# A gated cross-attention block in fp32 on one core: the first steps of stage 2 moved into attention's last block, and even score chunks

## The reference

```python
# x: (2, 2048, 512), context: (2, 77, 512); every product in fp32
h = layernorm(x)
z = self_attn(h, Wq1, Wk1, Wv1)        # one head, 2048 keys, causal, padding mask
x1 = layer_norm(h + z, ln1_g, ln1_b)
z = cross_attn(x1, ctx, Wq2, Wk2, Wv2) # 77 keys, mask by the count of non-zero scores in row 0
x2 = layer_norm(x1 + z, ln2_g, ln2_b)
z = relu(x2 @ fc1_w + fc1_b) @ fc2_w + fc2_b
x = x + tanh(g_xattn) * layer_norm(x2 + z, ln3_g, ln3_b)
# then the gated feed-forward with quantised weights: 512 -> 2048 -> 512, silu
x = x + tanh(g_ffn) * (x + 0.5 * ffn(layernorm(x)))   # ffn(...) as in the reference
```

## Time and profile before

| | |
|---|---|
| time, three runs | 1670.34, 1670.76, 1672.56 us |
| median | 1670.76 us |
| the profiled execution, its own time | 1670.44 us |
| its span in the profile | 1668.6 us |
| PE busy | 98% of the span |
| DVE, ACT, POOL busy | 51%, 34%, 22% |
| mean granted clock | 0.995 of full speed |
| chain that ended last | PE 91%, DVE 4%, POOL 2% |

### The profile page before, as it was taken

How to read it: one execution, slowest core, us unless ns; L and a number is a source line. 1 busy time by engine, 2 the same in 40 slices (tenths; PEclk the granted TensorE clock), 3 DMA queues, 4 the chain that set the end, 5 groups by cost and what they waited for, 6 DMA issues and landing times.

```text
span 1668.6 us, 20672 instructions
## 1 busy us (share of the span) xinstructions
PE 1636.9 (98%) x7746; PEld 1340.8 (80%) x7746; DVE 845.5 (51%) x1720; ACT 568.8 (34%) x990; POOL 368.9 (22%) x562
## 2 busy tenths in 40 slices
PE   8999999999999999899999899999999999999999
PEld 6887888877788888687878688888888888888887
DVE  6767443476664444688888955232333232333311
ACT  5432121134221212565566433232223222322322
POOL 1212101022210100488888801000000000000000
PEclk9999999999999999899999999999999999999999
DMA  6302110131221104554555432101010101010000
GB/s 210 105 22 95 44 51 26 40 114 57 70 76 39 38 26 140 163 165 152 164 164 158 126 115 69 45 1 51 1 51 1 51 1 51 1 51 1 26 1 26
DMA packets 66760, 116.19 MB, mean 70 GB/s; under 512 B 11185, under 2 KB 11185, under 8 KB 66507
## 3 DMA queue, kind: packets, MB, share of 16 engines
q1 hardware_dynamic: 64336, 110.36, 20.6%
q10 hardware_dynamic: 2325, 4.51, 0.8%
HBM read 80.00 MB, written 34.84 MB: 69 GB/s over the span
## 4 chain that ended last, share of the span: by engine, by line
PE 91%; DVE 4%; POOL 2%; issue 1%; ACT 1%; DMA 0%; SPq 0%; DVEq 0%; ACTq 0%
PE banks L694 86%; PE banks L704 3%; PE banks L881 2%; DVE split L1622 1%; DMA plain<-in_L_xattn_Wk 0%; POOL small L1486 0%; POOL split L1498 0%; DVE plain L1952 0%; DVE plain L1974 0%; POOL split L1505 0%; ACT plain L1193 0%; DVE split_q L1622 0%; ACT split L1086 0%; DVE plain L2156 0%; DVE plain L1662 0%
## 5 line engine op out<-in xcount | busy, mean ns | idle before, releaser
L694 PE MATMUL banks<-split_q,split 128*128 128x512 f32 x2328 | 571.3, 394 | 4.5 <-POOL split L1498 3.2
L694 PE MATMUL banks<-split 128*128 128x512 f32 (+4 forms) x2304 | 545.8, 386 | 9.6 <-DVE split L1622 6.5
L694 PEld LDWEIGHTS banks<-split_q,split 128*128 128x128 f32 x2328 | 431.3, 188 | 95.7 <-POOL split L1498 4.1
L694 PEld LDWEIGHTS banks<-split 128*128 128x128 f32 (+3 forms) x2304 | 414.1, 186 | 108.8 <-DVE plain L1952 9.0
L694 PE MATMUL banks<-split,split_q 128*128 128x512 f32 (+2 forms) x1728 | 394.8, 381 | 4.9 <-DVE split_q L1622 2.3
L694 PEld LDWEIGHTS banks<-split,split_q 128*128 128x128 f32 x1728 | 306.1, 189 | 61.3 <-DVE split_q L1622 3.5
L1622 DVE TENSOR_TENSOR split<-banks,split 128x512 fp32r<-128x512 f32 (+5 forms) x232 | 146.0, 638 | 154.5 <-ACT split L1086 153.6
L2121 DVE TENSOR_TENSOR split<-plain,split 128x512 fp32r<-128x512 f32 x128 | 88.5, 691 | 257.1 <-ACT split L1399 257.1
L1086 ACT ACTIVATE split<-banks 128x512 fp32r<-128x512 f32 (+5 forms) x232 | 123.8, 557 | 247.8 <-PE banks L881 199.5
L1393 ACT ACTIVATE plain<-banks,small 128x512 f32<-128x512 f32 x128 | 88.0, 688 | 289.1 <-PE banks L694 289.1
L1622 DVE TENSOR_TENSOR split_q<-banks,split_q 128x512 fp32r<-128x512 f32 x68 | 46.6, 686 | 222.0 <-ACT split_q L1086 222.0
(11 more groups left out here) (155 smaller groups left out, 1256.5 us busy)
## 6 DMA issues: line engine op xcount, KB each, us to landing
plain<-in_x SPq DMA_DIRECT2D x64, 256.0 KB, 2.7
xo_scratch<-plain SPq DMA_DIRECT2D x32, 256.0 KB, 2.3
x_scratch<-plain SPq DMA_DIRECT2D x32, 256.0 KB, 2.0
plain<-x_scratch SPq DMA_DIRECT2D x32, 256.0 KB, 3.0
tile_x<-xo_scratch SPq DMA_DIRECT2D x32, 256.0 KB, 3.1
xg_scratch<-tile_x SPq DMA_DIRECT2D x32, 256.0 KB, 2.0
out<-plain SPq DMA_DIRECT2D x32, 256.0 KB, 2.1
tile_x<-x_scratch SPq DMA_DIRECT2D x28, 256.0 KB, 3.8
```

The lines of the kernel that those rows point to most:

```text
L694: mm = nc.tensor.matmul(out, left(c, l), right(c, r), start=start and c == 0 and (l, r) == PASSES[0], stop=stop and c == chunks - 1 and (l ...
```

## The change

Five things change. (1) `span_of(i, c)`: scores of blocks 4, 8 and 12 are made in chunks of equal width (2 x 320, 3 x 384, 4 x 416) and not in 512s and a 128. Turns and values keep their chunks of 512. (2) The last block's list is written anew: Y1 stands before V1, K and Y3 and the first half of P follow, the other half of P stands behind the first turn of tile 1, and new letters are added: F splits of six of the eight row groups of fc1_w and fc2_w, J parts of `b1_shift`, U `probs`' turn and low part, y for all four turns of tile 1, H the four `cross_values(0, k)` with `add_z(0, k)`. (3) fc1_w and fc2_w get buffers of their own in `raw` (dead columns of xT) and are both loaded early, from SP, between N of tile 0 and V2; N of tile 1 is loaded early too; the vector loads wait for tile 0's additions. (4) `cross_values(0, k)` uses banks 6 and 5, and the addition of row block 15 (`sum_rows`) comes behind the four `add_z`. (5) Behind the list, PE does `cross_scores(1)` and then the turns of x2 with two parts of `b1_shift` between them, ACT takes `hi_x2` between the squares and the norms, DVE does block 15's end between the `lo_x2`, and the first `step2` has `mlp_in(0, 1)` ahead of `turn_scores(1)`.

```diff
+def span_of(i, c):
+
+    if i % 4:
+        return c * 512, width_of(i, c)
+    w = (i + 1) * P // chunks_of(i)
+    return c * w, w
...
             order += [("T", i, 0), ("T", i, 1), ("R", i, 0), ("V", i, 0), ("C", i, 0), end[0], ("Y", i, 0), ("T", i, 2),
-                      ("V", i, 1), end[1], ("Y", i, 1), ("Y", i, 2), ("V", i, 2), ("T", i, 3), ("Y", i, 3),
-                      ("P", i, 0), ("P", i, 1), ("K", i, 0), ("y", i, 0), ("y", i, 1), ("G", i, 0), ("V", i, 3),
-                      ("A", i, 0)]
+                      ("Y", i, 1), ("V", i, 1), end[1], ("Y", i, 2), ("K", i, 0), ("Y", i, 3), ("P", i, 0),
+                      ("y", i, 0), ("P", i, 1), ("F", i, 0), ("T", i, 3), ("F", i, 1), ("J", i, 0), ("y", i, 1), ("G", i, 0),
+                      ("V", i, 2), ("F", i, 2), ("U", i, 0), ("F", i, 3), ("y", i, 2), ("V", i, 3), ("F", i, 4), ("F", i, 5),
+                      ("y", i, 3), ("J", i, 1)]
+            order += [("H", i, c) for c in range(C)]
...
+                        for n, name in enumerate(("fc1_w", "fc2_w")):
+                            sp.dma_start(fc_raw[n], a[f"L0_xattn_{name}"].rearrange("(c p) n -> p c n", p=P)).then_inc(
+                                fcw_in[n], 16)
                         sp.dma_start(V2[0:SC].rearrange("p c h n -> p (c h n)").bitcast(F32), v_dram).then_inc(
                             cross_in, 16)
...
                     if i == NB - 1 and b + 1 == B:
-                        sp.wait_ge(z_free, 2 + B * NB)
+                        sp.wait_ge(tp_full, TURNS["p", b, i, 3] + 1)
+                        for k in range(BT):
+                            load_n(1, 1, k)
+                        sp.wait_ge(z_free, 2 + B * NB + BT)
...
+            def cross_values(t, k):
+                if k == 0:
+                    pe.wait_ge(tp_free, 2 + probs_at(t) + 1)
+                pe.wait_ge(z_free, z2_at(t, k) - 1 if t else B * NB + 1 + max(k - 1, 0))
+                product(PS[:, z2_bank(t, k)], lambda _, h: PT2[0:SC, h, k * P:(k + 1) * P],
+                        lambda _, h: V2[0:SC, t // TPB, h, :], 1, z2_full)
...
-            turn_x1(1, 2)
-            turn_x1(1, 3)
-            pe.wait_ge(fcw_in[0], 16)
-            b1_shift(0)
-            turn_probs(0)
-            b1_shift(1)
+            cross_scores(1)
             b1_shift(2)
+            turn_x2(0, 0)
+            turn_x2(0, 1)
             b1_shift(3)
-            pe.wait_ge(cross_in, 16)
-            for k in range(BT):
-                cross_values(0, k)
-            cross_scores(1)
-            for k in range(BT):
-                turn_x2(0, k)
+            turn_x2(0, 2)
+            turn_x2(0, 3)
             pe.wait_ge(fcw_lo, C)
             pe.wait_ge(b1_ready, 1)
...
             square_z(0, 0)
             square_z(0, 1)
             norm_z(0, 0)
             square_z(0, 2)
             norm_z(0, 1)
+            hi_x2(0, 0)
             square_z(0, 3)
             norm_z(0, 2)
+            hi_x2(0, 1)
             norm_z(0, 3)
-            hi_x2(0, 0)
-            hi_x2(0, 1)
+            hi_x2(0, 2)
+            hi_x2(0, 3)
+            hi_fc(6)
+            hi_fc(7)
...
+            sum_rows(NB - 1)
             stats_z(NB - 1)
-            split_fc1(range(C))
-            for k in range(BT):
-                add_z(0, k)
+            lo_x2(0, 0)
+            lo_x2(0, 1)
             end_b(NB - 1)
+            lo_x2(0, 2)
             dve.wait_ge(b1_full, 1)
             nc.vector.tensor_tensor(b1x, b1x, PS[:, 4, 0:C], ALU.add).then_inc(b1_ready, 1)
+            lo_x2(0, 3)
+            lo_fc(6)
+            lo_fc(7)
```

227 lines of the change are left out of this document (121 added, 106 removed).

## The result

| | before | changed |
|---|---|---|
| median of the runs, us | 1672.63 (8 runs, 1670.34 to 1674.91) | 1667.11 (8 runs, 1665.19 to 1669.80) |
| profiled execution, us | 1670.44 (span 1668.6) | 1669.80 (span 1668.0) |
| ratio to before | | 0.9972, 95% interval 0.9963 to 0.9981 |

The changed kernel is 0.28% faster: 4.7 us by the ratio (5.5 between the medians), where 2.5 were forecast, and just past the 0.2% that a measurement of it can tell from nothing. The range, 1664.3 to 1671.5, holds the median, and 1668.3 is 1.2 above it. That it comes so near is in part luck: the forecast started from 1670.76, the median of three runs, and the eight runs of before have 1672.63. The base was 1.9 too low and the gain too small.

What follows compares the result with a forecast made beforehand. PE, busy 98% of the span, was taken as the bound. From 1670.76 us: -1.7 chunks, -1.9 earlier `mlp_in`, +0.7 loads, +0.4 clock, together -2.5, gave 1668.3; range 1664.3 to 1671.5.

Steps and rivals of the forecast that it cites:

- Chunks: Stage 1 scores: even chunks save 0.42 at block 8 and 0.44 at block 12, 1.7 us over both batches.
- The two prices: Score chunks at blocks 8 and 12: one of 384 columns costs 2.19 us, one of 416 costs 2.35.
- The walk through the block: Last block, engines followed in five steps from the first turn of x1: `mlp_in` starts 1.9 us earlier.
- the four places named: PE's waits in the last block: 1.1 before Y1, 1.0 before P's second half, 1.6 on the exponential, 1.3 on `add_z`.
- the tail: Fifth step, first turn of x2 to `mlp_in`: 7.1 us instead of 5.3, giving back 1.8 of the 3.7 gained.
- The loads: fc1_w and fc2_w ahead of y0's rows on SP's queue: cost 0 to 2.0 us, taken as 0.7.
- The clock: Half clock when `mlp_in` starts: 2.0 us lost instead of 1.6, so 0.4 added.
- The rival with 0.14: Clock falls earlier as well, already at the last block's cross values, costing 2.7: 1671.0 us; chance 0.14.
- third and fourth steps: Last block, queues before the softmax, then additions: waits of 1.6 and 1.3; 3.7 us gained by the first turn of x2.
- free narrow chunks: Rival on stage 1 scores: evening out saves nothing, or DVE's extra maximum eats the gain: 1670.0 us; chance 0.08.
- the waits did not close: Rival on the last block: waits close, 1.6 less at `turn_probs`, and `mlp_in` at full clock, 2.0 less: 1664.7 us; chance 0.30.
- late rows: Rival on tile 1's rows: y0 waits until 672.6, 7.3 us beyond the count: 1675.6; chance 0.06. Wrong-sign: DMA wait over 3.

Runs made afterwards that it cites:

- a2_changed_again: The changed kernel with no edit, a second profiled execution beside the first; span 1665.4 us.
- e12: e11 plus ten overwritten products of 512 columns in the waits between the turns of x2; ratio to before 0.9972, median 1667.47 us.
- e10: Changed kernel with the fc loads behind y0's rows and the tail's ACT and DVE order turned round; ratio to before 0.9980, median 1669.19 us.
- e8: Changed kernel with later fc loads and ten overwritten products in PE's waits from the third turn of x2 to `mlp_in`; ratio to before 0.9977.
- e11: e10 plus the last two rows of one-column matmuls moved from the tail into earlier waits of PE; ratio to before 0.9965, median 1665.66 us.
- e13: Changed kernel with later fc loads, masks K behind Y3 and fc1_w's splits behind the softmax's scores; ratio to before 0.9990, median 1670.11 us.
- e1_chunks_only: Kernel before with even score chunks for blocks 4, 8 and 12 and nothing else; ratio to before 0.9984, median 1668.95 us.

## Why the prediction was right

**Chunks**: 1.7 forecast, 2.7 (1.2 to 4.2) measured alone, 1.9 in the trace of stage 1 (514.86 and 513.00 from block 4's scores to the turns ahead of the last block, 135.80 to 650.66 and 135.58 to 648.58). The two prices were right to 0.02. The surplus in the trace is the price of back-to-back chunks (2.12, taken as 2.19, and 2.28, taken as 2.35). Block 4 gave nothing, as forecast, and lost 0.1 in one batch and 0.3 in the other. The reason that I had given for such a loss, DVE's extra maximum, is not it: DVE makes that at 142.52, when PE's values have started at 142.34. They wait for a low part that DVE starts at 141.51, only 0.13 earlier than before, at the end of its own chain, while PE's chunks began 0.22 earlier. A narrow chunk of 128 columns costs 108 ns a matmul, and evening it out pays. The Trainium skill (TensorE: Matmul & The Clock Gate, Back-to-back issue gap) gives N / 2.4 + 2.5 ns for the isolated gap, 56 at 128 columns, and 81 ns for a stream of pairs of a load and a matmul. The Trainium skill (TensorE: Matmul & The Clock Gate, LDWEIGHTS (loading the stationary operand)) gives P / 1.2 ns for the load alone, 107 ns for 128 columns. The measured 108 lies at the last of these, so the load may be what a narrow chunk pays for. That isn't shown: the trace of before has each of these loads (24 of them from 188.6 to 192.6) at 187 to 192 ns, longer than the spacing, and no run here took the loads away.

**The walk through the block**: the waits came at four of the four places named, at sizes of 1.07 (forecast 1.1), 0.73 where no late rows hide it (1.0), 1.10 (1.6) and 0.65 (1.3). So none was larger than forecast, while the starts behind the last three, counted from the first turn of x1 in a2_changed_again, came within 0.3: 9.4 (forecast 9.3), 16.9 (17.0) and 24.1 (24.3). The chain of DVE and ACT that ends these waits was walked rightly; PE's own work ahead of the last two had been priced 0.3 to 0.4 too short. The first turn of x2 came 29.32 behind the first turn of x1 in a2_changed_again, forecast 684.9 - 655.67 = 29.2; the tail took 7.00, forecast 7.1; `mlp_in` 36.32, forecast 36.3. In the profiled execution of the changed kernel itself it came at 39.03, because of the loads and the early half clock.

**The loads**: the first rows were forecast 9.9 to 10.9 behind the first turn of x1; they came 10.1 behind it in the changed kernel, 8.5 in a2_changed_again and 7.8 in the block alone. Cost 0.7 with bounds 0 to 2.0; the traces have 1.2, 0 and 0.

**The clock**: half clock at `mlp_in`, as forecast, in every trace of a kernel with the new block but e12's. The 24 products lost 7.61 - 5.75 = 1.9 in the changed kernel, 1.4 in its second trace, 2.9 in the block alone; forecast 2.0. The reading of rows behind it was less exact: I had counted eight one-column matmuls in the tail, where the timeline has 16 (two rows of 8), and had said that turns and one-column matmuls preceded both falls of before, where only turns and waits preceded the second. The rival with 0.14, that the clock falls at the cross values too, is what the profiled execution of the changed kernel shows (6.02 instead of 4.57, 1.4 us), and it cost about as much as the load. It is no property of the kernel: a2_changed_again is the same code and hasn't got it. So this rival was no alternative to the forecast but something that differs from one execution to the next.

**What the sum left out.** Between the traces of before and a2_changed_again (spans 1668.6 and 1665.4) the gain is 3.2 and not 2.5. It is made of 2.1 ahead of the first turn of x1 (forecast 1.7; 0.2 of the 2.1 were there before the first changed chunk), 1.9 from there to `mlp_in` (forecast 1.9 less 0.7 for the loads, which cost nothing here), 0.2 given back up to the eight turns (forecast 0.4, for the clock) and 0.6 given back behind them, which had no term.

By the means of many runs the gain is 4.3: 1672.0 for the 89 runs of before beside the experiments, 1667.7 for the 18 of the changed kernel. The 1.1 that this has over 3.2 lies in the profiled execution of before, which was a fast one: 1670.44, 1.5 below the mean, where a2_changed_again's 1667.25 is 0.4 below its own. The 25 of the 89 runs with its mean clock of 0.995 average 1671.7. The forecast was worked out from that execution.

The granted clock doesn't explain the 1.1. Time does go with it in the runs of before (18 at 0.993 average 1673.1 us and 16 at 0.996 average 1671.0, 0.7 us for each 0.001), and the changed kernel has 0.9963 over its 18 runs where before has 0.9943. But the two traces differ by the same 0.002 (0.995 and 0.997; 17.1 and 10.2 us of half clock in all), so what the higher clock is worth is already in the 3.2. It is in the forecast too, whose third and fourth steps take out the long low stretch of before. Adding it to the sum would count it twice. What makes a usual execution of before slower than its trace stays open, since no trace shows such a run.

Of the rivals, free narrow chunks are refuted; the waits did not close, and where experiments closed them the time came back at half clock or at the next wait; late rows stayed at 1.97 and did not reach the 3 us that would have made it wrong.

## What to carry to other kernels

Price a narrow chunk of a score row by its own rows in the trace: at 128 columns a matmul cost 108 ns here and at 512 it cost 237, so the same columns in equal pieces are cheaper, wherever no wait stands behind them. Before crediting a shortened wait ahead of a stretch of half clock, mark a point behind that stretch: 1.46 us gained at the first product were 0.04 us some 18 us later. Where the effect sought is a few tenths of a per cent, take a second trace of the same kernel before explaining a row: one wait of 1.97 and one of 0.30 had the same code. And take one of before as well: the only one here was 1.5 us faster than the mean of its kernel.

## What of the hardware was not expected

- The stretch of half clock at the MLP's entry kept its place when PE's work in it was changed: 32.5 to 34.0 us behind the first turn of x1 and 6.8 us long, with PE busy 4.38 (a2_changed_again), 5.39 (e10) or 6.41 us (e8) of it. The Trainium skill (TensorE: Matmul & The Clock Gate, Part 4: PE-mode transpose) says that turns don't count as busy for the clock in the way that products do. The traces fit that: turns, most often with one-column matmuls, preceded it in the kernels in which it stayed. Moving the one-column matmuls away with the tail's order (e11) or adding products (e8) left it. With all of these together (e12) one trace has it at two other places with the same total of 6.7 us. Whether the edit did that isn't shown: the two traces of the changed kernel also have it at different places (679.55 and 689.80 in one, 686.05 alone in the other).
- The same start of the program was at half clock in two traces and not in the others. e13 had 3.35 us of it at 12.3 to 15.65 us of the span, behind 32 turns and a wait of 1.57 for DVE; e1_chunks_only had 6.75 us at 11.35 to 18.10, behind and among turns with waits of 0.68, 1.39 and 1.41. Before has turns with waits of 0.84 and 1.57 there and no fall. In e1_chunks_only this cost about 3.5 us (first turn of x1 at 657.11, in the changed kernel 653.57), most of the effect of the whole change.
- The latency of the same four row loads behind the same 2.1 MB differed by 1.6 us between two executions of one kernel (medians 10.2 and 8.6). The weights themselves landed alike in both, 7.8 and 10.5 us after their issue in one and 7.8 and 10.3 in the other, so the difference arose behind them; no run shows by what.
